# VectorE's order in an expert step: the copy of the last turned chunk and the normalise of the newest tile change places

## The reference

```
h   = gelu(x @ w1[e] + b1[e])          # 384 -> 64
out = (h @ w2[e] + b2[e]) * prob_max   # 64 -> 384
x   = x + out
```

## Time and profile before

| what | us |
| --- | --- |
| median of 3 runs | 2161.38 |
| lowest and highest | 2161.37, 2163.28 |
| the profiled execution | 2160.51 |
| its span | 2158.7 |
| busy in the span: TensorE | 2091.0 (97%) |
| VectorE | 1656.5 (77%) |
| ScalarE | 1491.7 (69%) |
| GpSimd | 1413.0 (65%) |

### The profile page before, as it was taken

The page is one execution under the profiler, slowest core; times in us unless marked ns, Lnnn a source line. Parts: engine busy times, 40 slices in busy tenths (PEclk is TensorE's granted clock), DMA queues, the critical chain, the costliest instruction groups (busy, mean ns, idle before and its releaser), DMA issues. The chain is left out here.

```text
span 2158.7 us, 56998 instructions
## 1 busy us (share of the span) xinstructions
PE 2091.0 (97%) x13580; PEld 2038.0 (94%) x13581; DVE 1656.5 (77%) x5452; ACT 1491.7 (69%) x3901; POOL 1413.0 (65%) x3348
## 2 busy tenths in 40 slices
PE   6999999999999999999999999999999999968997
PEld 5999999999999999999999999999999999957996
DVE  5777777777777777677777777777777777758997
ACT  4777767667776776676776776677776767637775
POOL 2556666666666666666666666666666666655887
PEclk9999999999999999999999999999999999978999
DMA  7101111211111111111111111111111111117995
GB/s 194 32 27 50 38 49 48 104 50 47 43 49 50 51 42 50 43 47 47 43 46 50 47 42 50 44 50 50 50 39 50 47 39 49 34 56 234 279 294 192
DMA packets 94261, 153.77 MB, mean 71 GB/s; under 512 B 17621, under 2 KB 70619, under 8 KB 93954
## 3 DMA queue, kind: packets, MB, share of 16 engines
q1 hardware_dynamic: 75844, 99.61, 16.0%
q0 software_dynamic: 17408, 50.62, 6.1%
q10 hardware_dynamic: 704, 0.10, 0.0%
HBM read 96.11 MB, written 57.32 MB: 71 GB/s over the span
## 5 line engine op out<-in xcount | busy, mean ns | idle before, releaser
L422 PE MATMUL bank<-wT_hi,hT_hi 128*128 128x384 f32 x2304 | 798.8, 347 | 11.3 <-issue 4.8
L424 PE MATMUL bank<-wT_hi,hT_lo 128*128 128x384 f32 x2304 | 774.2, 336 | 0.0
L423 PE MATMUL bank<-wT_lo,hT_hi 128*128 128x384 f32 x2304 | 773.1, 336 | 0.0
L422 PEld LDWEIGHTS bank<-wT_hi,hT_hi 128*128 128x128 f32 x2304 | 434.9, 189 | 20.5 <-ACT bank L622 12.4
L423 PEld LDWEIGHTS bank<-wT_lo,hT_hi 128*128 128x128 f32 x2304 | 435.2, 189 | 0.0
L424 PEld LDWEIGHTS bank<-wT_hi,hT_lo 128*128 128x128 f32 x2304 | 434.0, 188 | 0.0
L1173 POOL TENSOR_TENSOR hT_lo<-hT,hT_hi 128x384 fp32r<-128x384 f32 x256 | 261.5, 1022 | 22.9 <-ACT hT_hi L687 21.3
L682 ACT ACTIVATE hT<-bank 128x384 f32<-128x384 f32 x256 | 125.9, 492 | 203.0 <-PE bank L414 183.5
L658 ACT CAST right_hi<-bank 128x384 fp32r<-128x384 f32 x256 | 122.6, 479 | 173.9 <-PE bank L424 173.2
L1228 POOL TENSOR_SCALAR_AFFINE_SELECT deltaT_hi<-turned_hi 128x128 fp32r<-128x128 f32 x256 | 85.3, 333 | 211.8 <-ACT turned_hi L664 209.2
L414 PE MATMUL bank<-hT 128*128 128x128 f32 x1536 | 213.3, 275 | 0.0
(11 more groups left out here) (201 smaller groups left out, 5145.2 us busy)
## 6 DMA issues: line engine op xcount, KB each, us to landing
tok<-buckets SPq DMA_DIRECT2D x72, 388.0 KB, 4.5
x_in<-in_x_dram SPq DMA_DIRECT2D x128, 192.0 KB, 2.5
x_res<-in_x_dram SPq DMA_DIRECT2D x128, 192.0 KB, 2.4
adj_in<-in_adj_dram SPq DMA_DIRECT2D x128, 64.0 KB, 2.4
buckets<-pads SPq DMA_DIRECT2D x9, 388.0 KB, 4.9
out_dram<-out_rows,row_ids POOLq DMA_INDIRECT x144
buckets<-rows,dest_words POOLq DMA_INDIRECT x128, 2.7
w_top<-in_L_ffn_w_dram SPq DMA_DIRECT2D x2, 768.0 KB
```

The source lines that it names most:

```text
L422: pe.matmul(o, hi, w_hi, start=False, stop=False, skip_group_check=True)
L423: pe.matmul(o, hi, w_lo, start=False, stop=False, skip_group_check=True)
L424: last = pe.matmul(o, lo, w_hi, start=False, stop=(c == C - 1), skip_group_check=True)
```

## The change

In VectorE's step, `copy_last(i - 1)` is issued ahead of `normalise(i)` instead of behind it. Both keep their waits, operands and semaphores. No other engine's program changes. In step 0 there is no copy, and in the step after the last tile there is no normalise, so the order differs in 71 of the steps.

```diff
                     def step(i, k):
                         if there(i - DEPTH):
                             combine(i - DEPTH, (k - DEPTH) % RING)
+                        if there(i - 1):
+                            copy_last(i - 1, k - 1)
                         if there(i):
                             normalise(i, k)
-                        if there(i - 1):
-                            copy_last(i - 1, k - 1)
                         if there(i - 2):
                             gelu_high(i - 2, k - 2)
                             gelu_low(i - 2, k - 2)
```

## The result

The changed kernel took 2167.01 us (median of 8 runs, 2165.48 to 2170.08) against 2161.38 (8 runs, 2159.49 to 2163.28): +5.6 us, a ratio of 1.0026 with a 95% interval of 1.0017 to 1.0035. The range (2160.3 to 2167.5) held it, 0.5 us under its top. The forecast of +2.1 did not size it: its own range, 2161.5 to 2165.9, is missed. "Within 0.2%", which had 0.79 of the chance, is not what came by the median, though the interval's lower end does not rule it out.

The account below looks back on a forecast made before the run. TensorE paces the expert steps, VectorE has little to spare, GpSimd's stores set the end. Fill 1.06 plus boundaries 3.2 gives 4.3, less 2.18 of GpSimd's surplus lag: +2.1, 2163.5 us; range 2160.3 to 2167.5.

Parts of the forecast that it names:

- Within 0.2%: Whole run: time changes by less than 4.3 us, about what a measurement can tell from none; chance 0.79.
- rival B: Expert stage: later normalise holds up GpSimd's stores, 0.10 us in one store every other tile; +4.4 us, 2165.9; chance 0.12.
- signs of being wrong outright: Expert stage: its end moves by over 5 us, or a steady-step copy is found waiting for its transposes.
- Blocks: Loop bodies of 8 tiles in the expert stage: eight steps to take 21.7 to 22.0 us instead of 21.44.
- The ring and its room: Two-step wait loop through VectorE, TensorE, ScalarE: 5.00 us against TensorE's 5.30, room 0.30; the copy makes it 5.33.
- The block boundary: First step of each 8-tile loop body: with no room left, 0.40 us more each, +3.2 us over 8 boundaries.
- VectorE's jump: Loop body's first step: VectorE's combine comes 0.76 us after the gelu low part's start instead of 0.34, 0.42 lost.
- The fill: First steps of the expert stage: tile 1's normalise stands behind tile 0's waiting copy; +0.76 and 0.30, together +1.06 us.
- The upper bound of 1.9: First steps of the expert stage: delay reaches 1.9 us if TensorE's longer wait also puts off its clock rise.
- GpSimd's surplus lag: End of expert stage: stores trail combines by 3.06 us, least lag 0.88; the 2.18 surplus absorbs that much VectorE delay.
- B's recorded sign: GpSimd at tile 67: store lag stays at 2 us or more, with stores over 1.05 us.

Follow-up runs that it names:

- the opened ring: VectorE's two gelu parts one step later, against the kernel before: old order 2163.18 us, ratio 1.0007; changed order 2166.18 us, ratio 1.0017.
- the pair without stores: Expert-stage GpSimd stores dropped except the last tile's, against the kernel before: old order 2153.38 us, ratio 0.9962; changed order 2158.78 us, 0.9985.

## Why the prediction was right in kind and short in size

The range held, but on the side that had been widened for rival B, and one of the recorded signs of being wrong outright came true: the stage's end moved by more than 5 us (6.25 from the first normalise to the last store). Blocks took 21.9 to 22.2 us, where 21.7 to 22.0 stood. Part by part:

- **The ring and its room: right.** 5.33 us for two steps was forecast; without stores the changed order runs 2.655 a step, 5.31. Without stores undisturbed steps cost next to nothing, as forecast (0.3 us over the 40 steps away from the jumps of eight blocks); the copy gains nothing; the opened ring removes the loop's cost.
- **The block boundary: near in size, in part by luck.** Forecast 0.40 a block, 3.2 in all; with the stores the three steps at the jump pay 3.4, and without them the loop pays 4.05, 0.5 a block. The term counted VectorE's jump, which costs nothing in the pair without stores, and left out what costs there: TensorE's own jump, and the later gelu and high part in the body's first step.
- **The fill: mis-sized a little.** Forecast 1.06; measured 1.21, 1.45 without stores, 1.75 with the gelu parts late. In part TensorE's clock is in it: between 1956 and 1957 us it was granted 0.50 (1.2 GHz) in the changed order without stores and 1.00 (2.4 GHz) in the old one, after a fill in which TensorE waited for the second normalise. In the pair with the stores the same holds between 1955 and 1956 us: 0.50 in the changed kernel, 1.00 in the kernel before. The upper bound of 1.9 had that case.
- **Collisions with GpSimd: a term that the forecast had at nothing away from the jumps.** On VectorE's side they come on top of the ring: the loop costs 5.33 with the stores and 4.05 without, so 1.3 us, by difference of two pairs of traces. Counted by steps it is about 1.6, as the five steps away from the jump lose 1.9 with the stores and 0.3 without. The two need not agree, since VectorE's jump differs as well. What they do on GpSimd's side is in the point on rival B. In the Trainium skill, page "SBUF — State Buffer", section "SBUF: two separate sides", the port pair is locked by whichever of the two starts first, for a whole instruction. The trace agrees for the normalise and the high part, which are held when they start about 0.55 to 0.65 into a store (0.61 and 0.46 above), and disagrees on "whole instruction": the high part at 2078.76 ended at 2079.22, only 0.13 after the store's end at 2079.09, though it takes 0.29 when nothing holds it, so it was not kept out until then.
- **GpSimd's surplus lag: the step that failed.** "GpSimd's surplus lag takes 2.18 of it": it took 0.3 at the end. I had let the lag fall to the 0.88 of the first store. It stood at about 1.6 at the start of each block from the third to the seventh (1.57 at tile 56, where the kernel before had 3.01). Then the pause of 1.56 set it back to 2.5. Whether that pause belongs to the change was not tried; one trace has it.
- **Rival B came true on GpSimd.** Behind its first store GpSimd never waits for VectorE in either trace: at most 0.31 us of idle time stands before a store, that one pause apart. So its own time can be added up. From the first store of tile 0 to that of tile 67 it takes (2148.83 - 1962.32) / 67 = 2.78 a tile against 2.71, 4.9 us in all: 3.1 in the stores themselves (134 of them, 137.6 us against 134.5), 0.4 in the small additions, 1.4 in idle time, which is the pause. The 3.1 is what B priced at 3.4, and B's recorded sign, a lag of 2 or more with stores over 1.05, is there (2.63). I had given it 0.12. The ring still sets a floor: with the lag at its least of 0.88, tile 67 would have been stored 6.54 - 2.18 = 4.4 later than before, an estimate from these rows. GpSimd's own time put it at 6.1.

From the first normalise to the last store, by VectorE's side: the forecast 2.1, plus 0.15 for the fill, 0.85 for the loop without stores, 1.3 for the stores' part in the loop and 1.9 for the lag that was not absorbed, is the 6.3 of the profiled pair (the medians say 5.6).

## What to carry to other kernels

An instruction order whose steady step shows no loss can still have spent the room that a loop's jumps need: sum the ring of waits, and hold its room against every pause that some engine has once per body, each engine's jump included. A backlog on a third engine is a cushion only if that engine doesn't slow down with the others: add up its own time as well as its waits. And where a waiting instruction is moved ahead of one that is ready, the fill pays at once.

## What was not expected of the hardware

- In the changed kernel all 27 stretched normalises (SBUF to SBUF, one tensor in) start 0.55 to 0.59 us into a GpSimd indirect store of 1.0 us, and all 14 stretched high parts 0.64 to 0.75 us into one; they take up to 0.15 and 0.18 us more. A few others at these offsets keep their time. In the kernel before two of the six stretched normalises start earlier in the store, at 0.23 and 0.47 us. The gelu low part, with two SBUF inputs, kept 0.42 to 0.47 at every offset, in both.
- In the first step of a loop body, without stores, ScalarE's gelu starts 0.17 us behind the hidden matmuls instead of 0.04 and VectorE's high part 0.14 behind the gelu instead of 0.03, besides the jumps of VectorE (0.21 in the mean) and TensorE (0.27).
- Three chips gave 2162, 2215 and 2225 us for the same kernel; the expert stage starts between 1947.5 and 1952 us in every trace. The expert stage took about 271 to 289 us on the slower two, in the kernels traced there, instead of 203 to 217, with all engines standing for 1 to 4 us at a time. No row names the cause; it stays open. On the slowest the changed kernel cost +9.6 us instead of +5.6; the intervals overlap.
